# Mixture of experts on a Mamba/attention block: dense experts against tokens sorted into blocks of 128

## The chip, the core and the metric

The program runs on one NeuronCore of a Trainium2 chip. The core has five engines with their own instruction queues: TensorE (PE, matrix products, with its weight loads shown apart as PEld), VectorE (DVE), ScalarE (ACT), GpSimd (POOL) and SyncE (SP, which here only issues DMAs). The metric is the device time of one execution in microseconds (us), where less is better.

## The reference

The whole model is a state-space layer with a cross input, a quantised feed-forward layer, an attention layer and, last, a mixture of experts. Only the last layer is touched. x holds 4 batches of 512 tokens of 512 features, so 2048 tokens.

```python
scores = sigmoid(xt @ gate.T)                       # 2048 x 8
_, sel = top_k(scores + expert_bias, 2)             # two experts a token
top_scores = take_along_axis(scores, sel, axis=1)
order = argsort(sel.reshape(-1)); token_idx = order // 2; expert_ids = sel.reshape(-1)[order]
xb = (xt[token_idx] * top_scores[order]).astype(bfloat16)
for e in range(8):                                  # hidden size 256
    h = silu(xb @ w1[e].T) * (xb @ w3[e].T)
    oe = h @ w2[e].T
    out_r += where(expert_ids == e, oe, 0)
out = (silu(xt @ shared_w1.T) * (xt @ shared_w3.T)) @ shared_w2.T     # shared expert, f32
out = out.at[token_idx].add(out_r)
```

Here xt is the layer-normalised x, and the result is added to x. Each token is scaled by its score before it enters its two experts, so 4096 rows of work exist in all, out of the 16384 that eight experts on every token make.

## The kernel before

Everything ahead of the mixture of experts is one long schedule over the 4 batches. It ends with a last turn of attention, in which SP and POOL already load what the last layer needs: all expert weights in bf16 into `arena` (m_w1, m_w3, m_w2; POOL, L703), the shared expert's weights in f32 (into arena, wq and wo) and the first batch's x back from DRAM (`x3_load`, L544). The last SP load, s_w2 into wo, is issued after the last store of x.

The mixture of experts is then done batch by batch, 512 tokens at a time (`for_pairs`, L418, a loop over pairs of batches with the last pair written out). For a batch PE turns the normalised tokens into feature-major form (`xt_turned`, L1987: 4 groups of 4 transposes through PSUM tile pd, each drained by ACT at L1108), makes the 8 gate logits (32 records of 128x8, pd<-gateT,w2t), and ACT takes their sigmoid. DVE ranks the 8 biased scores of every token against each other (L1488 to L1505), and keeps a score where the rank is below 2 and zero elsewhere. So an expert that a token hasn't chosen sees that token as a zero row, and contributes zero.

For each expert e, DVE copies its gate column (`gcol`, L1508), PE spreads it over the partitions (`gates`, L2003, pd<-ident,gcol), DVE multiplies the whole batch by it into bf16 (`scaled_input`, L1512, 128x2048), PE computes the two up projections (`up`: 16 matmuls of 128x512), ACT applies Silu (L1120), DVE multiplies (L1518), and PE adds the down projection (`down`: 8 matmuls of 128x512) on top of what the shared expert and the experts before have left in the four PSUM banks `acc`. All matmuls go through the helper `mm`, L1548. The middle six experts stand in a hardware loop, where the weight address comes from a register. After the last expert DVE adds acc to x (L1541) and SP stores each quarter (L623). The next batch's layer norm (`moe_norm`) and transposes are woven into the last experts.

The order on each engine is the order in which the code of that engine's block is written. Nothing moves instructions between engines or reorders them; the engines meet at semaphores.

Of the kernel before, what the change touches and what calls it, by code (L numbers as in the profile page):

```python
# [13 lines left out]
BF16 = mybir.dt.bfloat16  # L14
ALU = mybir.AluOpType
# [4 lines left out]
P = 128  # L20
# [10 lines left out]
GH = 2  # L31
# [8 lines left out]
SAFE = 80.0  # L40

# [43 lines left out]
def program(nc, t):  # L85
    ctx = ExitStack()
    with ctx:
# [8 lines left out]
        x3_dram = nc.dram_tensor("x3_dram", (B, L, DM), F32).ap()  # L96
        kt_dram = nc.dram_tensor("kt_dram", (U_ALL, P, GH, L), F32).ap()
# [6 lines left out]
        tri = sb("tri", [P, E_, E_])  # L104
        minus_half = sb("minus_half", [P, 8])
# [108 lines left out]
        xbT = [qk_flat[:, i * NC * L:(i + 1) * NC * L].rearrange("p (c q) -> p c q", c=NC) for i in range(2)]  # L214

        x3 = [xs, xc]
        xn_moe = [w1t[:].rearrange("p c h -> p (c h)").bitcast(F32)[:, i * HID:(i + 1) * HID].rearrange("p (t d) -> p t d", t=NT) for i in range(2)]
        xnT_moe = [w2t[:].rearrange("p k d -> p (k d)").bitcast(F32)[:, i * HID:(i + 1) * HID].rearrange("p (c q) -> p c q", c=NC) for i in range(2)]
        gl = sb("gl", [P, 4, NT, E_])
        gcol = sb("gcol", [P, 2, NT])  # L220
        rk = sb("rk", [P, 2, E_, E_])
        hid_s = v_sb[:].rearrange("p t w -> p (t w)").rearrange("p (m q) -> p m q", m=MM)
        hid = [qkT_bf[:, i * HID:i * HID + MM * L].rearrange("p (m q) -> p m q", m=MM) for i in range(2)]
        sil = oT
        xo = hbuf[:, 1, 0:2 * DM].rearrange("p (s d) -> p s d", s=2)
# [9 lines left out]
        y_first = [ps[0], ps[1], po, pd]  # L235

# [65 lines left out]
        x3_in = [sem("x3_in0"), sem("x3_in1")]  # L302
# [7 lines left out]
        gb_full = sem("gb_full")  # L310
        gcol_done = sem("gcol_done")
        xb_done = sem("xb_done")
# [4 lines left out]
        xo_done = sem("xo_done")  # L317
        out_stored = [sem("out_stored0"), sem("out_stored1")]
# [99 lines left out]
        def for_pairs(eng, batch):  # L418


            with eng.Fori(0, B // 2 - 1) as j:
                for par in range(2):
                    batch(j * 2 + par, j, par, True)
            for par in range(2):
                batch(B - 2 + par, B // 2 - 1, par, par == 0)
# [10 lines left out]
        def _(sp):  # L436
# [4 lines left out]
                     (dtT, dram["dtT"]),  # L441
# [102 lines left out]
            def x3_load(b, par):  # L544
                sp.dma_start(x3[par][:], x3_dram[b].rearrange("(t p) d -> p t d", p=P)).then_inc(x3_in[par], 16)

            def turn(b, off, scan):
# [63 lines left out]
                sp.dma_start(x3_dram[b].rearrange("(t p) d -> p t d", p=P), xc[:]).then_inc(x3_stored, 16)  # L611
# [3 lines left out]
            sp.wait_ge(x3_stored, 16 * B + 16)  # L615

            def batch(b, j, par, follows):
                if follows:
                    sp.wait_ge(xo_done, NT * b + 1)
                    x3_load(b + 1, 1 - par)  # L620
                for k in range(NT):
                    sp.wait_ge(xo_done, NT * b + k + 2)
                    sp.dma_start(dram["out"][b].rearrange("(t p) d -> p t d", p=P)[:, k, :], xo[:, k % 2]).then_inc(out_stored[k % 2], 16)  # L623
            for_pairs(sp, batch)
            for i in range(2):
                sp.wait_ge(out_stored[i], 16 * B * NT // 2 + 16)
# [3 lines left out]
        def _(pool):  # L630
# [5 lines left out]
            def diagonals(s):  # L636

                if s == 0:
                    pool.wait_ge(const_in, 16 * 15)
# [44 lines left out]
            def turn(b, off, scan):  # L684
# [20 lines left out]
                def group(g):  # L705
                    G = b * NG + g
                    row_rms(G)
                    if is_first(g):
                        rstd(0 if scan else 3, 3 * b + 3)
                    if not scan:  # L710
                        expert_load(g)
# [3 lines left out]
            def batch(b, j, par, follows):  # L715
                if follows:
                    rstd(3, b + (3 * B + 1))
            for_pairs(pool, batch)


        @block.scalar
        def _(act):
# [139 lines left out]
            act.wait_ge(const_in, 16 * 15)  # L862
# [242 lines left out]
            def xt_out(b, par, k):  # L1105

                act.wait_ge(xt_full, b * NT + k + 1)
                nc.scalar.activation(xnT_moe[par][:, :, k * P:(k + 1) * P], pd[:].rearrange("p (c q) -> p c q", c=NC),  # L1108
                                     ACT.Copy).then_inc(xt_drained, 1)

            def batch(b, j, par, follows):
                X0 = b * (E_ + 1)
                act.wait_ge(logits_full, b + 1)
                nc.scalar.activation(gl[:, 0].rearrange("p t e -> p (t e)"), pd[:, 0:NT * E_], ACT.Sigmoid).then_inc(scored, 1)

                def silu(X):
                    for m in range(MM):
                        act.wait_ge(h1_full, 2 * X + m + 1)
                        act.wait_ge(hid_done, 2 * X + m + 1)
                        nc.scalar.activation(sil[:, m], px[0][:], ACT.Silu).then_inc(silu_done, 1)  # L1120
                silu(X0)
                with act.Fori(0, E_ - 1) as e:
                    silu(X0 + e + 1)
                if follows:
                    xt_out(b + 1, 1 - par, 0)
                silu(X0 + E_)
                if follows:
                    for k in range(1, NT):
                        xt_out(b + 1, 1 - par, k)
            for k in range(NT):  # L1130
                xt_out(0, 0, k)
            for_pairs(act, batch)
# [970 lines left out]
```

## Time and profile before

| | us |
|---|---|
| median of 3 runs | 2113.51 (2104.38 to 2113.51) |
| the profiled execution | 2109.74 |
| its span | 2108.1 |
| last layer in it, from the first transpose for it (1794.46) to the end | 313.6 |
| PE busy in the span | 1986.6 (94%) |
| mean granted TensorE clock | 0.963 of full |

The profile is of one execution, and its span is 1.6 us shorter than that execution's time. A busy PE includes the pipelined tail of a matmul, so two matmuls of 379 ns that start 0.215 us apart cost 0.215 us each. A granted clock of 1.00 is 2.4 GHz, one of 0.50 is 1.2 GHz. SPq stands for SP issuing a DMA; landing is when its semaphore has its last increment.

### The profile page before, as it was taken

Reading aid. Unit: us, or ns where it says so; the run is one execution under the profiler, and the core shown is the slowest. Engines: PE = TensorE matmul, PEld = TensorE weight load, DVE = VectorE, ACT = ScalarE, POOL = GpSimd, SP = SyncE. Lnnn points to the kernel's source line nnn. Section 1 sums busy time; section 2 is a strip of 40 time slices with the busy share of each in tenths; the row PEclk is TensorE's granted clock in tenths of the full one; section 3 lists DMA queues with packets and bytes.
Section 4 is the critical chain, followed back from the end, with each engine's and each line's share of the span. In section 5 each row is a group of like instructions: output and inputs, shape, how many; then the busy total and the mean of one; then the engine's idle time right before and its main releaser. Section 6 shows DMA issues by size and latency. Waiting matters only on the chain.

```text
span 2108.1 us, 24462 instructions
## 1 busy us (share of the span) xinstructions
PE 1986.6 (94%) x7508; PEld 1135.4 (54%) x7548; DVE 1462.6 (69%) x1762; ACT 1032.5 (49%) x2208; POOL 246.8 (12%) x124
## 2 busy tenths in 40 slices
PE   6899899999999989999998999988899999899998
PEld 2455445565654455656445665644556565454554
DVE  3799537999996699999758999993532333456554
ACT  4676435655653665656357655534444444121121
POOL 1002010111110021212001212100211010000000
PEclk8899899999999999999999999998999999999999
DMA  5264211222221122322202222222143332110100
GB/s 164 73 207 147 88 69 52 70 82 83 90 85 71 31 79 76 90 78 87 90 22 66 90 76 88 85 80 75 63 93 72 77 82 52 51 40 0 40 20 20
DMA packets 100788, 158.29 MB, mean 75 GB/s; under 512 B 9952, under 2 KB 53600, under 8 KB 100208
## 3 DMA queue, kind: packets, MB, share of 16 engines
q1 hardware_dynamic: 89136, 149.02, 22.0%
q0 software_dynamic: 10768, 6.82, 2.3%
q10 hardware_dynamic: 816, 1.57, 0.2%
q8 instruction: 40, 0.66, 0.1%
q14 instruction: 28, 0.23, 0.0%
HBM read 138.25 MB, written 25.43 MB: 78 GB/s over the span
## 4 chain that ended last, share of the span: by engine, by line
PE 60%; issue 25%; DVE 8%; ACT 3%; POOL 2%; DMA 1%; POOLq 0%; SPq 0%; ACTq 0%; DVEq 0%
PE ps L1548 21%; PE px L1548 13%; PE pp L1548 12%; PE po L1548 6%; PE pd L1548 6%; DVE arena L1212 2%; PE pp L1893 2%; DVE arena L1204 1%; ACT hbuf L1047 1%; ACT arena L783 1%; POOL rms_k L669 1%; DVE arena L1223 1%; POOL rms L660 0%; DVE xc L1404 0%; DVE arena L1230 0%
## 5 line engine op out<-in xcount | busy, mean ns | idle before, releaser
L1212 DVE TENSOR_TENSOR_SCAN arena<-arena 128x512 f32<-128x512 f32 x256 | 294.2, 1204 | 0.6
L1548 PE MATMUL ps<-qkT 128*128 128x512 f32 x512 | 256.4, 613 | 5.7 <-ACT hbuf L1047 3.0
L1047 ACT ACTIVATE hbuf<-ps,shift,rms_k 128x512 f32<-128x512 f32 x256 | 198.7, 778 | 123.8 <-PE ps L1548 116.2
L660 POOL TENSOR_TENSOR rms<-ssv,minus_half 128x4 f32<-128x4 f32 x64 | 154.0, 2407 | 808.5 <-ACT ssv L1023 808.5
L1548 PE MATMUL pp<-wq,xnT 128*128 128x256 f32 x1024 | 233.4, 382 | 2.9 <-issue 2.2
L1548 PEld LDWEIGHTS pp<-wq,xnT 128*128 128x128 f32 x1024 | 192.1, 190 | 41.0 <-issue 13.4
L1404 DVE SCALAR_TENSOR_TENSOR xc<-px,rden,xc 128x512 f32<-128x512 f32 x192 | 136.0, 738 | 85.0 <-PE px L1548 83.4
L1548 PE MATMUL px<-wo,oT 128*128 128x512 f32 x384 | 183.2, 599 | 0.7 <-DVE xc L1404 0.3
L783 ACT ACTIVATE arena<-arena,a_neg 128x512 f32<-128x512 f32 x256 | 163.3, 710 | 13.3 <-DVE arena L1190 7.3
L1548 PEld LDWEIGHTS ps<-qkT 128*128 128x128 f32 x512 | 91.7, 194 | 132.5 <-ACT hbuf L1047 70.6
L1548 PE MATMUL pp<-ctx_att,wk 128*128 128x512 f32 x256 | 134.3, 668 | 22.0 <-ACT ssv_k L845 6.4
L1120 ACT ACTIVATE oT<-px 128x512 f32<-128x512 f32 x72 | 43.0, 597 | 200.8 <-PE px L1548 200.8
L1548 PE MATMUL po<-hbuf,v_sb 128*128 128x512 f32 x256 | 130.7, 592 | 0.0
L1204 DVE TENSOR_TENSOR arena<-arena,bc 128x2048 f32<-128x2048 f32 x56 | 127.8, 2282 | 0.9 <-DVE v_sb L1172 0.6
L1548 PE MATMUL pd<-hbuf,v_sb 128*128 128x512 f32 x256 | 123.0, 603 | 0.0
L1223 DVE TENSOR_TENSOR arena<-arena,bc 128x2048 f32<-128x2048 f32 x52 | 118.8, 2284 | 0.0
L1336 DVE SCALAR_TENSOR_TENSOR hbuf<-px,fsc,ws 128x512 f32<-128x512 f32 x64 | 47.9, 750 | 98.4 <-PE px L1548 95.4
L1548 PE MATMUL ps<-wv,ctx_att 128*128 128x256 f32 x512 | 115.8, 379 | 0.0
L1230 DVE TENSOR_TENSOR arena<-arena 128x2048 f32<-128x2048 f32 x48 | 112.1, 2335 | 2.6 <-issue 0.3
L1418 DVE TENSOR_TENSOR dsum<-dsum,hbuf 128x512 f32<-128x512 f32 x128 | 88.6, 692 | 31.6 <-ACT hbuf L1047 25.6
L1548 PEld LDWEIGHTS ps<-wv,ctx_att 128*128 128x128 f32 x512 | 97.2, 190 | 13.4
L1548 PEld LDWEIGHTS px<-wo,oT 128*128 128x128 f32 x384 | 69.9, 189 | 58.9 <-issue 40.2
(211 smaller groups left out, 3087.0 us busy)
## 6 DMA issues: line engine op xcount, KB each, us to landing
bc<-bc_dram SPq DMA_DIRECT2D x56, 512.0 KB, 4.8
wo<-in_Wo SPq DMA_DIRECT2D x32, 512.0 KB, 3.6
wq<-in_Wq SPq DMA_DIRECT2D x32, 512.0 KB, 3.3
qkT<-kt_dram SPq DMA_DIRECT2D x32, 512.0 KB, 3.4
hbuf<-in_w SPq DMA_DIRECT2D x8, 1024.0 KB, 9.9
wk<-in_Wk SPq DMA_DIRECT2D x32, 256.0 KB, 2.8
wv<-in_Wv SPq DMA_DIRECT2D x32, 256.0 KB, 2.8
kt_dram<-xnT SPq DMA_DIRECT2D x14, 512.0 KB, 3.0
```

The lines of the kernel that those rows point to most:

```text
L660: nc.gpsimd.tensor_tensor(rms[:, j], ssv[:, j], half, ALU.pow).then_inc(rms_done, 1)
L783: nc.scalar.activation(dA[i][:, e], delta[:, e], ACT.Exp, scale=a_neg[:, e, bass.ds(g * GH + i, 1)]).then_inc(exp_done[i], 1)
L1047: nc.scalar.activation(pT[:, h, k], ps[s_use % 2][:], ACT.Exp, bias=shift[:, 0:1], scale=rms_k[:, bass.ds(G * (GH * NT) + (h * NT + k), 1) ...
L1120: nc.scalar.activation(sil[:, m], px[0][:], ACT.Silu).then_inc(silu_done, 1)
L1204: V.tensor_tensor(hb[i], du, bc_i[:, 0:1, :].broadcast_to((P, EC, L)), ALU.mult).then_inc(dbu_done[i], 1)
L1212: V.tensor_tensor_scan(hb[i][:, e], dA[i][:, e], hb[i][:, e], 0.0, ALU.mult, ALU.add).then_inc(scan_done[i], 1)
L1223: V.tensor_tensor(dst, hb[i], bc_i[:, 1:2, :].broadcast_to((P, EC, L)), ALU.mult).then_inc(hc_done[i], 1)
L1230: V.tensor_tensor(u, u, hb[i], ALU.add).then_inc(y_added, 1)
L1336: V.scalar_tensor_tensor(hbuf[:, k % 2, j * 512:(j + 1) * 512], bank, fsc[:, 0, 4, k:k + 1], ws1[:, j * 512:(j + 1) * 512], ALU.mult, ALU. ...
L1404: V.scalar_tensor_tensor(xc[:, k], px[bank][:], rden[:, h, k:k + 1], xc[:, k], ALU.mult, ALU.add).then_inc(px_drained[bank], 1)
L1418: V.tensor_tensor(dsum[:, h], dsum[:, h], pT[:, h, k], ALU.add).then_inc(ds_step[h], 1)
L1548: return nc.tensor.matmul(out, lhsT, rhs, start=first, stop=last, **kw)
```

## The change

The experts no longer see every token. Each token's two chosen experts are found as before, and then:

- `route_ranks` and `route_places` (DVE, with two small matmuls on PE, `places`) work out for each token its place among its expert's tokens. Each expert has its own region of 2048 + 128 rows in a DRAM tensor `xg_dram`.
- ACT scales the token-major rows by their score into bf16 (`routed_out`, 8 activations a batch), and POOL writes them to their places by indirect DMAs of 128 rows of 1 KB (`scatter`, 8 a batch, 32 in all). SP fills 128 rows behind each expert's last token with zeros.
- `block_tables` (DVE) turns the counts into a table: for each of 40 blocks of 128 rows, the expert's index (read into PE registers, six values for four blocks) and the first row (read into SP registers, four values for four blocks). 40 is the most that 4096 rows can need; unused blocks work on row 0 with expert 0.
- The 40 blocks run through a loop of ten turns with four blocks each. SP loads a block of 128x512 bf16 from xg_dram into one of four buffers, PE transposes it (`block_turned`), DVE copies it to SBUF (`block_x`), PE does the up projections (`block_up`: 16 matmuls of 128x128), ACT and DVE make the hidden values, PE does the down projection (`block_down`: 2 matmuls of 128x512), ACT copies it out as bf16 (`block_out`), SP stores it to `og_dram`.
- When all 40 blocks are stored, POOL gathers each token's two result rows (`gather`, 32 indirect DMAs), and DVE adds both to x (`final`).
- The shared expert is computed for batches 0 and 1 ahead of the blocks and for 2 and 3 behind them. All four batches of x are kept in SBUF. Layer norm of batch 1 moves into the last turn of attention, and two more constants are loaded at the start.

The core of the diff:

```diff
+NB = 40
+REGION = B * L + P
-                    x3_load(0, 0)
+                    for i in range(B - 1):
+                        sp.dma_start(x3[i], x3_dram[i].rearrange("(t p) d -> p t d", p=P)).then_inc(x3_in[i], 16)
...
+            def block_load(q, row):
+                sp.dma_start(xblk[q], xg_dram[bass.ds(row, P), :]).then_inc(xblk_in[q], 16)
+            def block_store(q, row):
+                sp.dma_start(og_dram[bass.ds(row, P), :], oblk[q]).then_inc(oblk_stored[q], 16)
+            rows = row_values(sp_tbl[0:1, 0, :])
+            for q in range(4):
+                block_load(q, rows[q])
+            def blocks(i, first, last):
+                if not last:
+                    rows = row_values(sp_tbl[0:1, bass.ds(i + 1, 1), :].rearrange("p o n -> p (o n)"))
+                for q in range(4):
+                    sp.wait_ge(bo_out, i * 4 + q + 1)
+                    block_store(q, i * (4 * P) + q * P)
+                    if not last:
+                        sp.wait_ge(bt_full, i * 4 + q + 1)
+                        block_load(q, rows[q])
...
+            def scatter(b):
+                for s in range(2):
+                    for k in range(NT):
+                        pool.wait_ge(routed_done, 2 * NT * b + s * NT + k + 1)
+                        nc.gpsimd.indirect_dma_start(
+                            out=xg_dram[:, :], out_offset=bass.IndirectOffsetOnAxis(ap=idx[:, b, s, k:k + 1], axis=0),
+                            in_=routed[b % 2][:, s, k], in_offset=None).then_inc(scattered[b % 2], 16)
...
+            for q in range(4):
+                pool.wait_ge(oblk_stored[q], 16 * NB4)
+            pool.wait_ge(table_step, TS + 4)
+            for b in range(B):
+                gather(b)
...
+            def block_out(j, slot, q, turns, head):
+                act.wait_ge(bo_full, j + 1)
+                if not head:
+                    act.wait_ge(oblk_stored[q], 16 * turns)
+                nc.scalar.activation(oblk[q], pp[slot][:], ACT.Copy).then_inc(bo_out, 1)
...
+            def final(b):
+                dve.wait_ge(g_in[b], 16 * 2 * NT)
+                dve.wait_ge(y_done, NT * b + NT)
+                for s_ in range(2):
+                    for k in range(NT):
+                        if s_:
+                            dve.wait_ge(fin_step, 2 * NT * b + k + 1)
+                        V.tensor_tensor(x3[b][:, k], x3[b][:, k], g_of[b][:, s_, k], ALU.add).then_inc(fin_step, 1)
...
+            hidden(2)
+            shared_out(2)
+            final(0)
+            hidden(3)
+            final(1)
+            shared_out(3)
+            final(2)
+            final(3)
...
+            def block_turned(j, slot, q, turns, head):
+                pe.wait_ge(xblk_in[q], turns)
+                for c in range(NC):
+                    m = nc.tensor.transpose(xT_ps[slot][:, c * P:(c + 1) * P], xblk[q][:, c * P:(c + 1) * P], ident_bf[:])
+                m.then_inc(bt_full, 1)
+            def block_up(j, slot, e, head):
+                pe.wait_ge(bt_out, j + 1)
...
+                for i, w in enumerate((m_w1, m_w3)):
+                    for m_ in range(MM):
+                        at_ = (i * MM + m_) * P
+                        for c in range(NC):
+                            m = mm(px[slot][:, at_:at_ + P], w[:, e, c, m_ * P:(m_ + 1) * P], xTs[slot][:, c * P:(c + 1) * P], c == 0, c == NC - 1,
+                                   skip_group_check=True)
+                m.then_inc(bh_full, 1)
+            def block_down(j, slot, e, head):
+                pe.wait_ge(bhid_done, j + 1)
...
+                for m_ in range(MM):
+                    m = mm(pp[slot][:], hT[slot][:, m_ * P:(m_ + 1) * P], m_w2[:, e, m_], m_ == 0, m_ == MM - 1)
+                m.then_inc(bo_full, 1)
+            def blocks(i, first, last):
+                e = expert_values(pe_tbl[0:1, bass.ds(i, 1), :].rearrange("p o n -> p (o n)"))
+                for q in range(4):
+                    if not (last and q == 3):
+                        block_turned(i * 4 + (q + 1), (q + 1) % 2, (q + 1) % 4, (i + (q + 1) // 4) * 16 + 16, first and q == 0)
+                    if not (first and q < 2):
+                        block_down(i * 4 + (q - 2), q % 2, e[q], first)
+                    block_up(i * 4 + q, q % 2, e[2 + q], first and q < 2)
```

On PE, in the loop over experts before, one expert begins like this. ISA is a register instruction that sets the weight address; qk_raw is the scaled input, arena the expert's weights.

```order
L2008 ISA [waits xb_done]
L1548 ISA [waits silu_done]
L1548 MATMUL px<-qk_raw,arena 128x512
L1548 ISA
L1548 MATMUL px<-qk_raw,arena 128x512
```

On PE in the loop over blocks now, one block's turn begins like this. hbuf is the loaded block in the transposes (po<-ident_bf,hbuf) and its transposed copy in the up projection (px<-hbuf,arena); dsum is the hidden value of an older block.

```order
L2363 MATMUL po<-ident_bf,hbuf 128x128 [waits bt_out,xblk_in2]
L2363 MATMUL po<-ident_bf,hbuf 128x128 x3
L1837 ISA [waits bo_out,bhid_done]
L1837 MATMUL pp<-arena,dsum 128x512
L1837 ISA
L1837 MATMUL pp<-arena,dsum 128x512
L1837 ISA [waits bhid_done,bt_out]
L1837 MATMUL px<-hbuf,arena 128x128
```

In the turn of block s, PE transposes block s+1, does the down projection of block s-2 and then the up projection of block s. The transposes wait for a load (xblk_in), and the down projection stands behind them in the queue.

On SP before, the loop over batches loads one batch of x and stores four quarters of another (xo_done is DVE's last addition).

```order
L614 DMA wo<-in_s_w2T 128x2x512
L421 UNCONDITIONAL_BRANCH [waits x3_stored]
L545 DMA xc<-x_dram 128x4x512 [waits xo_done]
L623 DMA out<-hbuf 128x512 [waits xo_done] x4
L545 DMA xs<-x_dram 128x4x512 [waits xo_done]
```

On SP now, one turn of the block loop begins like this; og_dram<-hbuf is a block's store, hbuf<-xg_dram the load of the block four further on.

```order
L674 TENSOR_LOAD wk
L702 ISA
L692 ISA [waits bo_out]
L692 DMA og_dram<-hbuf 128x512
L689 ISA [waits bt_full]
L689 DMA hbuf<-xg_dram 128x512
L702 REGISTER_ALU
```

A load is issued behind the store of the block four before it, and that store waits for the block's down projection to be copied out (bo_out).

## Rows read from the trace of the kernel before

**Rows 1.** page, part 1: busy us, share of the span, instructions
```profile
PE 1986.6 (94%) x7508; PEld 1135.4 (54%) x7548; DVE 1462.6 (69%) x1762; ACT 1032.5 (49%) x2208; POOL 246.8 (12%) x124
```

**Rows 2.** busy us of each engine by stretch; PEclk is the granted clock
```profile
core 0: us, PE busy (x) PEld busy (x) DVE busy (x) ACT busy (x) POOL busy (x), PEclk, DMA share, GB/s
1850.00:1900.00 50.00, 49.16 (x218) 25.86 (x220) 24.70 (x48) 11.73 (x19) 0.00 (x0) 0.97 0.12 42
1900.00:1950.00 50.00, 49.51 (x226) 24.18 (x230) 32.54 (x45) 10.48 (x18) 1.01 (x1) 1.00 0.00 0
```

**Rows 3.** timeline of one expert: start us, us, engine, line, operation, count
```profile
2067.14 2.84 PE L1548 MATMUL px<-qk_raw,arena 128*128 128x512 bf16 x12
2067.34 2.29 DVE L1512 TENSOR_TENSOR qk_raw<-w2t,pd 128x2048 bf16<-128x2048 f32 x1 [1.31 <-PE pd L2003]
...
2072.84 0.38 PE L1548 MATMUL px<-qk_raw,arena 128*128 128x512 bf16 x1
```

**Rows 4.** timeline: turning tokens, logits, shared up and down
```profile
1794.46 0.60 PE L1987 MATMUL pd<-ident,w1t 128*128 128x128 f32 x4
...
1795.84 0.63 PE L1987 MATMUL pd<-ident,w1t 128*128 128x128 f32 x4 [0.78 <-ACT w2t L1108]
...
1802.52 6.91 PE L1548 MATMUL pd<-gateT,w2t 128*128 128x8 f32 x32 [3.24 <-DMA wo<-in_s_w2T]
...
2030.70 3.74 PE L1548 MATMUL pd<-gateT,w2t 128*128 128x8 f32 x32 [0.69 <-ACT w2t L1108]
...
2039.50 1.88 PE L1548 MATMUL px<-w2t,wq 128*128 128x512 f32 x4
...
2057.57 2.74 PE L1548 MATMUL ps<-wo,v_sb 128*128 128x512 f32 x6
```

**Rows 5.** groups of instructions, 1815 to 2108: busy us, mean ns, idle before
```profile
L1120 ACT ACTIVATE oT<-px 128x512 f32<-128x512 f32 x72 | 43.0, 597 | 200.8 <-PE px L1548 200.8
...
L1518 DVE TENSOR_TENSOR qkT<-oT,po 128x512 bf16<-128x512 f32 x32 | 22.0, 687 | 23.5 <-PE po L1548 23.5
```

**Rows 6.** timeline of weight loads: fixed addresses, then addresses from a register
```profile
186.63 0.10 PEld L1548 LDWEIGHTS px<-ident_bf,qkT 128*128 128x128 bf16 x1
186.69 0.10 PEld L1548 LDWEIGHTS px<-minus_bf,qkT 128*128 128x128 bf16 x1
...
1838.75 0.10 PEld L1548 LDWEIGHTS px<-qk_raw,arena 128*128 x1 [0.40 <-issue]
1838.87 0.10 PEld L1548 LDWEIGHTS px<-qk_raw,arena 128*128 x1
1839.00 0.10 PEld L1548 LDWEIGHTS px<-qk_raw,arena 128*128 x1
```

**Rows 7.** DMA issues: engine, count, KB each, median us from issue to landing
```profile
wq<-in_Wq SPq DMA_DIRECT2D x32, 512.0 KB, 3.3
...
wk<-in_Wk SPq DMA_DIRECT2D x32, 256.0 KB, 2.8
...
out<-hbuf SPq DMA_DIRECT2D x16, 256.0 KB, 2.2
...
arena<-in_m_w3T POOLq DMA_DIRECT2D x8, 256.0 KB, 5.7
...
bc_dram<-arena SPq DMA_DIRECT2D x4, 64.0 KB, 1.6
...
gateT<-in_gateT SPq DMA_DIRECT2D x1, 16.0 KB, 2.0
```

**Rows 8.** timeline: SP's issue of a load that had waited for PE
```profile
1727.49 0.59 PE L1548 MATMUL pp<-wq,xnT 128*128 128x256 f32 x2
...
1728.28 0.37 SPq L470 DMA_DIRECT2D wq<-in_Wq  x1
```

**Rows 9.** busy us by stretch, where PE waits often
```profile
50.00:60.00 10.00, 4.55 (x36) 3.88 (x36) 9.79 (x7) 7.82 (x10) 0.00 (x0) 0.58 0.57 174
260.00:270.00 10.00, 6.45 (x17) 3.77 (x16) 0.00 (x0) 1.44 (x3) 0.00 (x0) 0.50 0.58 180
```

**Rows 10.** timeline: POOL's issues of direct loads
```profile
1730.64 0.79 POOL L703 DMA_DIRECT2D arena<-in_m_w1T  x1
1731.42 0.76 POOL L703 DMA_DIRECT2D arena<-in_m_w3T  x1
```

More of the change, by code:

```diff
@@ L14 @@
 BF16 = mybir.dt.bfloat16
+I32 = mybir.dt.int32
 ALU = mybir.AluOpType
@@ L416, in is_last, with for_blocks @@
             return isinstance(g, int) and g == NG - 1
[L418 to L425, printed above, removed]
+        def for_blocks(eng, blocks):
+            blocks(0, True, False)
+            with eng.Fori(1, NB4 - 1) as i:
+                blocks(i, False, False)
+            blocks(NB4 - 1, False, True)
         def for_groups(eng, group):
@@ L624, in _, with row_values @@
-            for_pairs(sp, batch)
-            for i in range(2):
-                sp.wait_ge(out_stored[i], 16 * B * NT // 2 + 16)
+            def row_values(ap):
+                _, values = nc.values_load_multi_w_load_instructions(
+                    ap, engines=[mybir.EngineType.SP], min_val=0, max_val=E_ * REGION - P,
+                    skip_runtime_bounds_check_because="rows are worked out from counts of at most B * L tokens an expert")
+                return values
+            sp.wait_ge(zero_set, 1)
@@ L1113, in batch @@
                 act.wait_ge(logits_full, b + 1)
[L1114 to L1123, printed above, removed]
@@ L2062, in _ @@
+            for b in range(2):
+                xt_turned(b)
+                logits(b)
+            places(0)
             pe.wait_ge(mw_in, 16 * (3 * E_ + 1))
-            pe.wait_ge(sw_in, 32)
             for i in range(2):
@@ L2067, in _ @@
                 pe.wait_ge(px_drained[i], turn_of(B - 1, OFF_LAST)[0]["px"] + HALF_LAST["px"])
-            for_pairs(pe, batch)
+            up(0, 0)
+            up(0, 1)
+            places(1)
+            down(0)
+            for b in range(2, B):
+                xt_turned(b)
+                logits(b)
+            places(2)
+            up(1, 0)
+            places(3)
+            pe.wait_ge(gate_step, GS * 3 + 13)
+            pe.wait_ge(y_done, NT)
+            mm(acc[3][:, 0:E_], ones[:], before[:, B * NT], True, True).then_inc(count_full, 1)
@@ new lines, in _, with expert_values @@
+            up(1, 1)
+            down(1)
+            def expert_values(ap):
+                _, values = nc.values_load_multi_w_load_instructions(
+                    ap, engines=[mybir.EngineType.PE], min_val=0, max_val=E_ - 1,
+                    skip_runtime_bounds_check_because="the count of experts that end by a block, times whether the block is one of theirs")
+                return values
+            def block_turned(j, slot, q, turns, head):
+                pe.wait_ge(xblk_in[q], turns)
+                if not head:
+                    pe.wait_ge(bt_out, j - 1)
+                for c in range(NC):
+                    m = nc.tensor.transpose(xT_ps[slot][:, c * P:(c + 1) * P], xblk[q][:, c * P:(c + 1) * P], ident_bf[:])
+                m.then_inc(bt_full, 1)
```

562 lines of the change are left out of this document (390 added, 172 removed).

## The prediction, made before the changed kernel ran

> **What bounds the kernel now.** I read the page's part 1 first: PE is busy for 94% of the span [rows 1]. By stretches the last layer is no different: PE 49.2 and 49.5 us of 50 at a clock of 0.97 and 1.00, DVE 25 to 33, ACT 11 [rows 2]. So in this layer every microsecond taken off PE counts, if nothing takes its place. The timeline then gives the price of its parts. One expert on one batch: its twelve first matmuls start at 2067.14, those of the next expert at 2072.84, so 5.70 us [rows 3], and DVE's 2.29 us scaling lies beside them. 8 experts x 4 batches x 5.70 = 182 us of the 313.6 us from 1794.46 to the end. The other 131 us are turning tokens, logits, the shared expert and the end.
>
> **What goes.** All 182 us, gate spreading and scaling included. Before, the first logits also waited 3.24 us for s_w2, in the row of 1802.52 [rows 4]; now only `down` waits for it.
>
> **The blocks: what one costs PE.** With a fixed weight address a load and a matmul of 128 columns start 0.06 us after the pair before; with an address from a register the weight loads start 0.12 and 0.13 us apart [rows 6]. In the old loop 0.12 was hidden, because a matmul of 512 columns lasts 0.215 us. Now it isn't: 16 x 0.125 = 2.0 us for the up projections. The transposes (fixed) take 4 x 0.06 = 0.25, the down projection 2 x 0.215 + 0.1 = 0.5, waits and registers 0.2: 3.0 us a block. For 40 blocks that is 120 us against 182. ACT needs 0.60 for copying 512 columns out [rows 5] and about 0.4 for Silu on 256; DVE about 0.65 and 0.45. Neither decides.
>
> **The blocks: what one costs in latency.** The load of block j+4 is issued only after the store of block j, which waits until block j's down projection is copied out. PE does that down projection in the turn of block j+2 and wants block j+4 at the start of the next turn; the down projection of block j+1 stands behind those transposes. So from one down projection to the next there is a closed circle:
> - transposes 0.25, down 0.5, the array's tail 0.2 (a matmul of 215 ns is shown as 379), a wake-up 0.1: 1.05 us at full clock;
> - ACT's copy 0.60 [rows 5];
> - SP awake 0.2 us after the last releaser (PE ended at 1728.08, the issue began at 1728.28), the store's issue 0.37 [rows 8], the second wait and register 0.1: 0.7;
> - the load, from issue to landing. 512 KB take 3.3, 256 KB 2.8, 16 KB 2.0 [rows 7]. 128 KB on that line are 2.3 to 2.4; with a store of 128 KB just ahead of it in the same queue I take 2.5.
>
> Sum 4.85 us. The up projections (2.0 us) lie inside the load's time. The clock raises it: in stretches where PE is busy for 4.6 or 6.5 us of 10, the granted clock was 0.58 and 0.50, which is the 1.2 GHz level for most or all of it [rows 9]. Here PE would be busy for 3.0 of 4.9 us. At half clock transposes and down take 0.7 us more; with a part of that I take P = 5.0 us a block. Bounds: 2.0 for the load and full clock, 4.2; 2.9 for the load and half clock all the way, 5.9. PE reads six register values from SBUF every four blocks, and SP four. No row shows such a read; between nothing and the smallest load that a row has (2.0 us), it fits into PE's 2.0 us of waiting a block, so I take 0 and keep 0 to 0.5 us a block.
>
> The Trainium skill ("TensorE: Matmul & The Clock Gate", HAM oscillation) says that a matmul loop which waits for a DMA in every turn keeps falling back to 1.2 GHz. Rows 9 agree that the clock falls where PE waits. Followed fully it would make P 5.5 us and the time 2175. The same notes ("DMA: Bandwidth & Descriptors", Latency and other measured facts) give a register load from memory a floor of about 600 ns, and "Runtime: NRT & Kernel Launch" about 200 ns a register; by that estimate PE's six are 1.2 us, hidden at P = 5.0 and showing only if PE bounds.
>
> From the first block's transposes to the end of the last down projection: 5 us to the first down, 36 P = 180 (the last four blocks need no further load), 5.5 for the last turns. 190 us, against 182 before. The 62 us that PE is spared turn into waiting.
>
> **Ahead of the blocks.** Everything from 1794.46 is now serial on PE: 4 batches turned at 4 x 1.40 us = 22 (1794.46 to 1795.84 is one [rows 4]); logits 3.7 to 6.9 us each [rows 4], 4 x 6 = 24, the clock being low behind them; shared expert of batches 0 and 1, up 32 records and down 16, eight records in 3.4 us [rows 4], 20.6 a batch = 41. Added waits: down(0) behind DVE's `route_places`(1) and `hidden`, 3.5; places and counts, handing pd back, 4; down(1) behind DVE's table (20 small operations of some 0.25 us), 3. Half clock on part of this, 7. Sum 105, so PE could begin the blocks at 1899. Queued behind these waits are only the blocks. The old kernel wove turning and ranking into its experts, where it cost little. Layer norm of batch 1 in the last turn of attention is hidden by DVE's idle half; the other cover, three loads of 1 MB in place of one, lies ahead of loads that are due 20 us later. Two more constants at the start: two issues, +1.
>
> POOL's indirect DMAs appear in no row. A direct one costs POOL 0.79 us to issue [rows 10] and lands after 5.7 when three are queued [rows 7]; I take 1.2 us each, nearer to the direct one, bounds 0.8 and 2.5. Then the 8 of a batch are 10 us. By the same sum the places of batch 3 are known at 1887; POOL is at batch 2 until 1889, ends batch 3 at 1899, which lands 2.5 later, and reading rows and loading the first block take 4 more: 1905. So the scatter sets the start, 111 us after 1794.5, bounds 95 to 125.
>
> **Behind the blocks.** PE computes the shared expert for batches 2 and 3: 2 x 20.6 + 2 x 0.9 of waiting for `hidden` = 43. POOL begins to gather when the last store has landed, 0.65 + 0.2 + 1.8 = 2.7 us after the last down projection (64 KB stored in 1.6, 256 KB in 2.2 [rows 7]); 32 x 1.2 = 38, landed at 43.5. DVE adds in its written order: final(1), 8 x 0.69 = 5.5 [rows 5], stands ahead of shared_out(3), which ends at 45.5; final(2) and final(3) 5.5 each, 56.5; the last store 2.2 [rows 7]: 58.7.
>
> **Sum.** 1794.5 + 111 + 190 + 58.7 + 1 = 2155 of span, against 2108. With 1.6 outside it, 2157; the runs shown lie from 5 under to 4 over the profiled execution, so 2157 stands as the forecast: 47 us or 2.2% slower. The change would pay only with P below 3.7 us.
>
> **Rivals.**
> - *PE bounds the blocks, faster.* The load lands before PE wants it, so P is PE's own 3.0 to 3.3 us. For it: 3.0 us of PE work a block is well counted, and DMA queues are nearly empty here (DMA share 0.12 and below [rows 2]). Against: the circle above needs the load to land in 0.7 us, and no load in rows 7 is below 2.0. It decides wherever the circle is below 3.7. Time: 36 x (5.0 - 3.0) = 72 less, 2085. Chance 0.14; with partial forms, 0.18.
> - *GpSimd bounds the ends, slower still.* An indirect DMA costs 2.5 us. The scatter of the last batch ends 18 us later, the gather takes 80 us instead of 38, so the last addition ends at 93 instead of 58.7: 2157 + 52 = 2209. For it: 128 separate rows each, made by an engine that needs 0.79 us even for a plain load. Against: nothing measured. Chance 0.13.
> - *Even.* P of 3.6 to 3.9 with the rest as summed: 2106 to 2118. Chance 0.06.
>
> My forecast has 0.63. Its own range is 2125 to 2195 (36 x 0.9 us on the block price, 15 on the front, combined). The range given, 2095 to 2210, adds the nearer part of both rivals. Slower by over 0.5% (about the smallest change a measurement of this kernel tells) 0.76, within 0.06, faster 0.18.
>
> **What would show it.** In the block stage the transposes (po and pd from ident_bf) idle on the DMA hbuf<-xg_dram, 4.2 to 5.9 us apart, PE busy for 60% and a clock well below 1. Wrong if they are about 3 us apart with no wait for a DMA: then the load's path was too dear. The chain at the end should be DVE additions behind the gather; if POOL issues are above 1.55 us each, they set the end. The front should last 95 to 125 us from the first transposes for this layer to the first block. The forecast is wrong as a whole if the span from the first block to the last down projection is below 145 us.

## The result, and the profile after

The changed kernel takes 2143.49 us (median of 4, 2141.89 to 2147.66) against 2112.14 for the kernel before beside it: a ratio of 1.0159, 95% interval 1.013 to 1.0189. It is slower, by 1.6% where 2.2% was forecast. The profiled spans are 2142.3 and 2108.1 us. PE is busy for less time and waits more:

```profile
PE 1940.1 (91%) x7519; PEld 1144.1 (53%) x7551; DVE 1399.0 (65%) x1759; ACT 1047.2 (49%) x2252; POOL 309.6 (14%) x189
```

That is 46 us less of busy PE than in [rows 1], and 34 us more of span. By stretches, the block stage:

```profile
core 0: us, PE busy (x) PEld busy (x) DVE busy (x) ACT busy (x) POOL busy (x), PEclk, DMA share, GB/s
1900.00:1950.00 50.00, 33.45 (x244) 24.23 (x245) 10.85 (x28) 9.23 (x20) 0.00 (x0) 0.69 0.18 56
1950.00:2000.00 50.00, 30.96 (x227) 22.55 (x230) 8.13 (x22) 10.43 (x22) 0.00 (x0) 0.69 0.19 58
2000.00:2050.00 50.00, 31.91 (x232) 23.27 (x232) 7.65 (x21) 10.51 (x22) 0.00 (x0) 0.66 0.19 58
```

Where [rows 2] had PE at 49 us of 50 and a clock of 0.97 and 1.00, it now has 31 to 33 at 0.66 to 0.69. What it waits for is in the answer for the transposes of the blocks:

```profile
its engine sat idle before it (us, times) until:
  DMA hbuf<-xg_dram: 114.5, 66
  issue: 15.1, 8
  DVE wv L1761: 4.9, 2
```

The 114.5 us are of two rows that wait side by side, the matmuls and their weight loads. The view of the loads (`xg_dram`) tells them apart:

```profile
  PE pd L2363: 30.4, 19
  PE po L2363: 30.4, 18
```

So PE itself waited 60.8 us for loads, in 37 waits. One turn of the circle follows, with the lines of weight loads and of VectorE left out:

```profile
1993.77 0.60 PE L2363 MATMUL pd<-ident_bf,hbuf 128*128 128x128 bf16 x4 [1.50 <-DMA hbuf<-xg_dram]
1994.17 1.06 PE L1837 MATMUL pp<-arena,dsum 128*128 x2
1995.02 1.91 PE L1837 MATMUL px<-hbuf,arena 128*128 128x128 bf16 x16
1995.35 0.60 ACT L1271 ACTIVATE hbuf<-pp 128x512 bf16<-128x512 f32 x1 [2.66 <-PE pp L1837]
1996.12 0.36 SPq L692 DMA_DIRECT2D og_dram<-hbuf  x1
1996.66 0.33 SPq L689 DMA_DIRECT2D hbuf<-xg_dram  x1
...
1998.86 0.40 PE L2363 MATMUL po<-ident_bf,hbuf 128*128 128x128 bf16 x4 [1.93 <-DMA hbuf<-xg_dram]
1999.31 0.38 PE L1837 MATMUL pp<-arena,dsum 128*128 x1
1999.73 0.60 ACT L1271 ACTIVATE hbuf<-pp 128x512 bf16<-128x512 f32 x1 [2.38 <-PE pp L1837]
2000.50 0.35 SPq L692 DMA_DIRECT2D og_dram<-hbuf  x1
```

Read it as a chain: transposes at 1993.77, ACT's copy 1.58 later, store 0.77 later, load 0.54 later, the next transposes 2.20 later, 5.09 us in all, with down at half clock (1.06 for two matmuls). The next turn has them at full clock (one of the two records is missing), and ACT's copy follows after 0.87 instead of 1.58: a turn that is 0.71 shorter, 4.4 us. The up projections (1.91) end long before the load has landed. The first row below gives the starts of the first and the last of the 40 stores, the others the DMAs' times from issue to landing (the last number):

```profile
L692 SPq DMA_DIRECT2D og_dram<-hbuf x40: 332/355/361, 1910.9 to 2086.4; - x40
```

```profile
hbuf<-xg_dram SPq DMA_DIRECT2D x40, 128.0 KB, 2.1
og_dram<-hbuf SPq DMA_DIRECT2D x40, 128.0 KB, 1.7
```

The last three intervals need no load and are 5.8 us together; the 36 before are 169.8 us, 4.72 each. The two ends of the last layer follow: GpSimd's last eight scatters (the second number is the median in ns), then from the timeline the start of the blocks and the end.

```profile
L807 POOL DMA_INDIRECT xg_dram<-qkT,wv x8: 956/956/978, 1890.0 to 1898.8; - x8
```

```profile
1901.86 1.94 SPq L689 DMA_DIRECT2D hbuf<-xg_dram  x4
...
1903.78 0.19 DVE L1761 TENSOR_TENSOR wv<-wk,wv 128x32 int32<-128x32 f32 x1
1904.05 0.38 PE L2363 MATMUL po<-ident_bf,hbuf 128*128 128x128 bf16 x4 [2.03 <-DVE wv L1761]
...
2089.09 0.99 POOL L814 DMA_INDIRECT w1t<-og_dram,wv  x1 [189.29 <-DMA og_dram<-hbuf]
2090.39 0.96 POOL L814 DMA_INDIRECT w1t<-og_dram,wv  x1 [0.30 <-issue]
...
2121.32 0.69 DVE L1769 TENSOR_TENSOR v_sb<-oT,po 128x512 f32<-128x512 f32 x1 [6.12 <-PE po L1837]
...
2121.93 4.99 DVE L1783 TENSOR_TENSOR ws<-ws,w1t 128x512 f32<-128x512 f32 x8
...
2128.08 0.94 POOL L814 DMA_INDIRECT qk_raw<-og_dram,wv  x1 [0.30 <-issue]
...
2129.86 4.90 DVE L1783 TENSOR_TENSOR bc<-bc,w2t 128x512 f32<-128x512 f32 x8
2134.67 4.90 DVE L1783 TENSOR_TENSOR xc<-xc,qk_raw 128x512 f32<-128x512 f32 x8
```

An indirect DMA takes POOL 0.95 us and the next starts 0.30 later: 1.25 to 1.27 from one to the next. The last addition ends 11.5 us after the last gather is issued. The row of 1904.05 names VectorE's L1761 as what PE waited for, but in the kernel PE waits there for the first load and for the table of blocks. The table was done at 1892.31 (L1749) and the load landed at 1903.92, so it was the load.

### The profile page after: what moved, and what is told of

It reads as the page before. It is cut to its first block, busy times and chain, and to the rows that moved or that the text cites. A ratio compares the mean times of both kernels' runs of the same rounds, so it can differ in the third digit from the quotient of the medians.

```text
span 2142.3 us, 25171 instructions
## 1 busy us (share of the span) xinstructions
PE 1940.1 (91%) x7519; PEld 1144.1 (53%) x7551; DVE 1399.0 (65%) x1759; ACT 1047.2 (49%) x2252; POOL 309.6 (14%) x189
## 4 chain that ended last, share of the span: by engine, by line
PE 62%; issue 16%; DVE 10%; ACT 5%; DMA 4%; POOL 1%; SPq 1%; ACTq 0%; DVEq 0%; POOLq 0%
PE ps L1837 20%; PE pp L1837 14%; PE px L1837 13%; PE pd L1837 7%; PE po L1837 5%; DMA hbuf<-xg_dram 4%; DVE arena L1368 2%; PE pp L2182 2%; DVE arena L1360 1%; ACT hbuf L1271 1%; ACT hbuf L1160 1%; ACT arena L896 1%; DVE arena L1379 1%; SPq L692 1%; PE pd L2281 1%
## 5 line engine op out<-in xcount | busy, mean ns | idle before, releaser
L1144 ACT ACTIVATE qk_raw<-pp,rms 128x128 f32<-128x128 f32 x256 | 72.9, 368 | 48.8 <-POOL rms L746 48.5
```

What stands on the lines that cost most here:

```text
L1144: m = nc.scalar.activation(qraw[:, k, h * D:(h + 1) * D], pp[bank][:, i * GW + h * D:i * GW + (h + 1) * D], ACT.Copy, scale=rms[:, j, h, i ...
```

## The experiments

My theory was the circle: block j+4's load stands behind block j's store in SP's order. Its rivals were a slow DMA path whoever asks for it, PE's work or its clock, and GpSimd at the two ends. The kernel before ran beside each group of kernels. It took 2107.2 us beside the first four kernels, and 2107.5 to 2109.3 beside the others. The first four ran on one chip (A), the next seven on another (B), the last on a third (C); which one had the changed kernel's own run isn't known. That matters below.

**Loads ahead of stores.**

```
 for q in range(4):
-    sp.wait_ge(bo_out, i * 4 + q + 1)
-    block_store(q, i * (4 * P) + q * P)
     if not last:
         sp.wait_ge(bt_full, i * 4 + q + 1)
         block_load(q, rows[q])
+    if not (first and q < 2):
+        sp.wait_ge(bo_out, i * 4 + q - 1)
+        block_store((q + 2) % 4, i * (4 * P) + (q - 2) * P)
...
```

(Behind the loop, the last two blocks are stored.)

> SyncE's loop is turned round: it loads block j+4 as soon as block j is turned, and stores block j-2 behind it, so that no load waits for a store of its own or a later block. Circle theory (the block period of 4.7 us is down, ACT's drain, SP's store and load issues and the load's 2.1 us landing, one behind the other): the circle opens, the waits of the block transposes on the loads vanish, and the period falls to TensorE's own work, 0.25 to 0.5 for turning, 0.5 for down, 2.0 for up and 0.15 to 0.2 for its share of the register load that is now bare: 3.0 to 3.3 us. 36 periods x 1.5 us = 50 to 60 us less than the changed kernel: about 2085 to 2095 us, below the kernel before. Rival 1 (the loads are late because the DMA queue or the memory is slow, whoever asks): the period stays above 4.3 us and the time above 2128. Rival 2 (TensorE's half clock in this stage sets the period): the clock stays at 0.65 to 0.70 and the period at or above 4.3 us.

Measured: 2083.94 us, 0.9895 of before (0.9873 to 0.9916). The stores, the transposes' waits, and the engines by stretch:

```profile
L692 SPq DMA_DIRECT2D og_dram<-hbuf x40: 332/355/362, 1911.0 to 2027.9; - x40
```

```profile
  issue: 20.7, 18
  DMA hbuf<-xg_dram: 3.2, 3
```

```profile
1950.00:2000.00 50.00, 44.82 (x354) 32.62 (x357) 12.32 (x33) 16.18 (x33) 0.00 (x0) 0.90 0.27 85
```

That is 1 us below the band I gave. The stores are 39 intervals of 3.00 us instead of 4.50 (here and below all 39 are counted alike). The row for the DMA fell from 114.5 to 3.2 us, and PE's own part of it from 60.8 to 2.6, though a load still takes 2.0 to land and 85 GB/s are moved instead of 58. So the DMA path was not slow, it was asked late. The clock rose from 0.69 to 0.90 once PE had work, with nothing changed but SP's order. Both rivals fall.

**The load ahead of the store, with the same waits.**

```
 sp.wait_ge(bo_out, i * 4 + q + 1)
-block_store(q, i * (4 * P) + q * P)
 if not last:
     sp.wait_ge(bt_full, i * 4 + q + 1)
     block_load(q, rows[q])
+block_store(q, i * (4 * P) + q * P)
```

> The waits of SyncE's loop stay as they are; only the issue of the load of block j+4 stands ahead of the store of block j. Circle theory: the store's issue and the step behind it (0.35 + 0.2 us) leave the circle, so the period falls by 0.5 us (4.7 to 4.2) and the time by 36 x 0.5 = 18 us, to about 2125 us. Rival (TensorE's work or its clock sets the period): nothing changes, 2143 +- 4 us.

Measured: 2126.58 us, 1.0087 of before (1.007 to 1.0104), 16.9 less than the changed kernel.

```profile
L692 SPq DMA_DIRECT2D og_dram<-hbuf x40: 333/356/1362, 1915.0 to 2070.2; - x40
```

The 39 intervals take 155.2 us, 3.98 each against 4.50: one issue out of the circle is worth 0.52 us a block, as in the chain above (store to load, 0.54). Nothing else was changed, so the circle is closed through SP's order, and taking out a part shortens it by that part. The block stage is 20.3 us shorter and the whole only 16.9, because in the profiled execution the blocks began 3.6 us later (1907.64 for 1904.05). That was late already in the work ahead of them: ACT's wait of 5.8 us for the logits ended at 1865.19 instead of 1861.61.

**Gate and up weights at a fixed address, alone and with the loads ahead.**

```
-m = mm(px[slot][:, at_:at_ + P], w[:, e, c, m_ * P:(m_ + 1) * P], ...
+m = mm(px[slot][:, at_:at_ + P], w[:, 0, c, m_ * P:(m_ + 1) * P], ...
```

All blocks then go up through expert 0, whatever their own expert is.

> The gate and up weights of every block are read at expert 0's fixed address instead of at the register's (so all blocks go up through expert 0; down keeps its register). TensorE's 16 matmuls of a block take about 0.9 to 1.1 us instead of 2.0. Circle theory: the up step lies beside the load's landing, so the period stays within 0.2 us of 4.7 and the time within 8 us of 2143 (2135 to 2147). Rival (TensorE's work sets the period): the period falls by 0.9 us to 3.8, the time by 33 us to 2110.

> Both at once: loads ahead of stores, and gate and up weights at expert 0's fixed address. Circle theory: with the circle open TensorE's work counts, so the fixed address now gives what it gave nothing for alone: 0.7 to 1.0 us a block below the loads-ahead kernel, a period of 2.0 to 2.4 us, a time of about 2050 to 2065 us. Rival (something beside TensorE, as the chain turn, copy, up, silu, multiply, down, sets the period at 3 us or more once the loads are in time): the same time as loads ahead alone.

Measured: 2133.90 us alone (1.0123, 1.0106 to 1.014), 2028.28 us with the loads ahead (0.9629, 0.9604 to 0.9653). The stores, alone and then together:

```profile
L692 SPq DMA_DIRECT2D og_dram<-hbuf x40: 332/355/362, 1909.3 to 2081.5; - x40
```

```profile
L692 SPq DMA_DIRECT2D og_dram<-hbuf x40: 332/355/412, 1910.3 to 1972.4; - x40
```

Alone the interval goes from 4.50 to 4.42; with the loads ahead from 3.00 to 1.59. The same edit is worth 0.08 us a block inside the circle and 1.41 outside it. That is the plainest proof of what bounds which kernel. Two sizes missed. Alone the median fell 9.6 us, 1.6 beyond my band. In the profiled executions the block stage gave 3.4 of it and the work ahead 1.6; the rest isn't in that execution, which took 2139.38. Together I expected 2050 to 2065, having priced the address at 0.9 us a block.

The 1.41 us are not all the address. With the loads ahead, three transposes of four start 2.6 to 3.0 us apart and the fourth about 3.99, because PE's queue stands still for 1.35 us at the turn of the loop (its branch, the load of six registers of 0.59, some register steps). With the fixed address too, the intervals are 1.55 to 1.70 and the fourth 1.73: the same turn, with a register load of 0.75, lies beside matmuls that are already queued. So about 1.2 us of the 1.41 are the weights' addresses, and the other 0.2 to 0.3 is the turn of the loop, now hidden.

**Half the gathers.** GpSimd fetches only the rows of the first choice, and the additions use them twice:

```
-for s in range(2):
+for s in range(1):
     for k in range(NT):
         nc.gpsimd.indirect_dma_start(out=g_of[b][:, s, k], ...
```

> The changed kernel with 16 indirect gathers instead of 32: the rows of the second choice are not fetched, and the final additions take the first choice's rows twice. GpSimd is done 20 us earlier. Theory (the end is set by the shared expert's chain of batches 2 and 3 on TensorE and by VectorE's order behind it; the last gather lands only just in time at 2130 us): final(2) still starts 44.4 us after the last block, so the time moves by 0 to 1.5 us, 2142 to 2144. Rival (GpSimd's gathers set the end, as the case of slow indirect DMAs in the prediction had it): the time falls by 5 to 20 us. A little in between would say that the landing of batch 3's rows is what final(3) waits for.

Measured: 2152.85 us (1.0225, 1.0201 to 1.0249): above the changed kernel, which neither theory nor rival had. From the last store's issue to the end it is 55.9 us (2090.4 to 2146.3) with 16 gathers, as with 32 (2086.4 to 2142.3). So GpSimd doesn't set the end, which was the question. The extra time was at another place, below.

**Eight blocks' experts in one register load** (on top of loads ahead; PE's loop over 8 blocks, its table of 10 values a row).

```
-for q in range(4):
+for q in range(8):
     ...
-        block_down(i * 4 + (q - 2), q % 2, e[q], first)
-    block_up(i * 4 + q, q % 2, e[2 + q], first and q < 2)
+        block_down(i * 8 + (q - 2), q % 2, e[q], first and q < 4)
+    block_up(i * 8 + q, q % 2, e[2 + q], first and q < 2)
```

> The loads-ahead kernel with TensorE's table of experts read for eight blocks at a time (10 registers a load, 5 loads in the loop) instead of for four (6 registers, 10 loads). In the loads-ahead trace TensorE stands still for 1.25 us at each load, where a block's turning starts 4.0 us after the one before instead of 2.75. If the price is that of a load: 5 x 1.25 = 6 us less, 2078 us. If it is that of a register (60 before, 50 now): 1.25 / 6 x 10 = 2 us less, 2082 us. If the stall has nothing to do with the load (a jump of the loop, say) it also halves with the count of turns of the loop, as in the first case, which this run can't tell apart.

Measured: 2116.98 us (1.0045, 1.0028 to 1.0062). PE's register loads, first in the loads-ahead kernel, then in this one, and its stores:

```profile
L2357 PEldq TENSOR_LOAD <-wk x9: 588/592/612, 1914.8 to 2013.9; - x9
```

```profile
L2357 PEldq TENSOR_LOAD <-wk x5: 1081/2412/2427, 1940.6 to 2037.9; - x5
```

```profile
L692 SPq DMA_DIRECT2D og_dram<-hbuf x40: 332/356/362, 1925.9 to 2043.1; - x40
```

The 39 intervals take 117.2 us against 116.9: no gain where I expected 2 to 6 us. There are half as many loads, of 10 values each. They alternate: three of the five take 2.4 us and the two between them 1.08, instead of 0.59. Rows of the table now start 40 bytes apart and not 32; whether that makes every second load long wasn't tested.

**Another order of additions at the end** (on top of loads ahead).

```
 final(0)
-hidden(3)
+hidden(3, (0,))
 final(1)
-shared_out(3)
+hidden(3, (1,))
 final(2)
+shared_out(3)
 final(3)
```

> The loads-ahead kernel with another order on VectorE at the end: final(1) goes between the two halves of hidden(3), and final(2) ahead of shared_out(3), both in gaps of 6 us in which VectorE stood still. The last batch's rows land 44.6 us after the last block and shared_out(3) is done by 44.3, so the last additions end at 49.5 and the store at 51.7 instead of 56.8: 5 us less, 2079 us. Rival (the gathers land later than I read them, or the order delays TensorE's chain by more than it gives): within 2 us of 2084.

> Loads ahead, eight blocks' experts a load, and the new order at the end, together; nothing is left out of the computation. The three act in different places (each block, each loop turn, the end) and should add up: 2084 - 6 - 5 = 2073 us, 1.6% below the kernel before. If one hides another (the register load was partly beside something else, or TensorE's chain at the end moves with the clock), 2076 to 2080.

Measured: 2112.82 us (1.0024, 1.0011 to 1.0036) and 2112.41 us (1.0022, 1.0006 to 1.0037), 34 and 39 us over expectation. The piece that the order touches did what it should: from the second product of hidden(3) to the end it is 21.0 us in the changed kernel (2121.32 to 2142.3) and 16.3 in both of these (2094.49 to 2110.8, 2091.67 to 2108.0), 4.7 less. No median shows that gain: on this chip the loads-ahead kernel without the new order took 2107.62 (below), and the one with it 2112.82.

**Weights moving, tokens loaded** (with the three edits above).

```
-for m_ in range(MM):
-    at_ = (i * MM + m_) * P
-    for c in range(NC):
-        m = mm(px[slot][:, at_:at_ + P], w[:, e, c, m_ * P:(m_ + 1) * P], xTs[slot][:, c * P:(c + 1) * P], ...
+for c in range(NC):
+    m = mm(px[slot][:, i * MM * P:(i + 1) * MM * P], xTs[slot][:, c * P:(c + 1) * P], w[:, e, c], ...
...
+for m_ in range(MM):
+    m = nc.tensor.transpose(hT_ps[slot][:, m_ * P:(m_ + 1) * P], hmid[slot][:, m_ * P:(m_ + 1) * P], ident_bf[:])
```

> As the three together, but gate and up are computed with the tokens' block as the loaded operand and the expert's weights as the moving one: 8 matmuls of 256 columns instead of 16 of 128 whose loaded operand stood at the register's address; the product then needs two more turnings of 128x128 and a copy of 128x256 on VectorE before down. Nothing is left out. If the cost of the register's address is that of each loaded weight tile (0.125 us apart instead of 0.056), a block loses 16 x 0.125 = 2.0 us and gets 8 x 0.11 + 0.2 = 1.1 us: 0.9 us less a block, 40 x 0.9 = 36 us less, about 2040 us, unless the longer way (turn, copy) leaves a wait of 0.2 to 0.4 us in each block (then 2048 to 2055). Rival (a register's address costs the same wherever it stands, for each column that it moves): no gain, 2073 us or more.

Measured: 2096.58 us (0.9937, 0.9919 to 0.9955). That is 15.8 under the three together beside it, where 36 less was expected, and far over the 2040 to 2055 expected of the time.

**What was late in the last five.** The traces of these five have a place at about 1898 us where VectorE starts 9 us after the matmul that it waits for should have ended, though PE's own records run on at their usual spacing. All but the half-gather kernel have a second place near the end, where ACT and VectorE wait for the shared expert's products: from the last block store to the end they take 18 to 24 us longer than the loads-ahead kernel's 55.9 (less the 4.7 where the order is new). To tell chip from program:

> The loads-ahead kernel once more, beside the next. The last five kernels were all 8 to 35 us over what was expected of them, and their traces show why only in part: TensorE's results come 9 us late at 1898 us (VectorE waits for the last gate and up product), and in four of the five 21 us late behind 2064 us, while the block stage between runs as expected. They ran on another chip than the first four. If the late results belong to that chip, this kernel has them wherever the next one has them, and takes about 2112 us there, or neither has them and it takes 2084 us again. If they belong to the changes of the last kernels (the order of the program, its length), this kernel takes 2084 us whether the next one is late or not.

> The kernel with the weights as the moving operand once more, on the same chip as the loads-ahead kernel. Chip theory: its stalls (9 us at 1898 us and about 20 us near the end) are there or away together with those of the loads-ahead kernel: about 2096 us with them, about 2066 to 2070 us without; the difference to the loads-ahead kernel is 15 to 18 us in both cases. Program theory: 2096 us, above the loads-ahead kernel's 2084.

> The changed kernel itself once more, to compare the kernels of the last three calls with. Chip theory: if it falls on the chip on which TensorE's results came late, it has the 9 us at 1898 us, as the kernel with half the gathers had there (2152.9), and up to 15 us more near the end, where the full 32 gathers run beside the shared expert: 2153 to 2168 us; on another chip it takes 2143 us as before. Rival (the half-gather kernel was slower for a reason of its own): 2143 us on any chip. The block period is 4.7 us in every case.

Measured: loads ahead on chip B 2107.62 us (1.0009, 0.9994 to 1.0024) where it had 2083.94 on A; weights moving 2086.83 (0.9916, 0.9888 to 0.9943), with both late places, where 2096 was expected with them and 2066 to 2070 without; the changed kernel, on C, 2148.08 (1.0186, 1.0166 to 1.0206), with none of the late places. The changed kernel with all its gathers was not run on B, and why the half-gather kernel has only the first place isn't explained. The loads-ahead kernel on A has no such wait; on B:

```profile
ACT oT L1246 <- remote: 36.8, 2, 29.6
DVE v_sb L1773 <- remote: 27.2, 2, 19.7
```

("remote" is a release that nothing in the trace explains.) SP is slow at the first place too, where it issues the eight stores of zeros; A, then B:

```profile
L682 SPq DMA_DIRECT2D xg_dram<-dsum x8: 332/337/529, 1889.6 to 1893.7; - x8
```

```profile
L682 SPq DMA_DIRECT2D xg_dram<-dsum x8: 3/356/695, 1885.9 to 1898.4; - x8
```

The block stage is the same on both: 116.9 us for 39 intervals. The kernel before shows none of it in its times on B. What the late places have in common isn't settled. The executions also reach the last layer at different times: ACT's wait for the logits ended at 1861.63 in the loads-ahead kernel on A and at 1857.69 on B. The first store on B is at 1915.1 for 1911.0, so the first place cost 8.1 us and not 4. Counted so, it cost 10.4 to 10.6 in the kernels with half the gathers, eight a load, new order and three together.

So the loads-ahead kernel's gain of 23 us over before is that of chip A, and it is nothing on B. On B the weights-moving kernel was 20.8 us below it. Of the 18.9 between the profiled executions, 16.5 are 39 intervals of 2.57 instead of 3.00 (stores from 1911.0 to 2011.4) and 4.1 lie ahead of the first store; from the last store to the end it took 1.7 longer (72.0 for 70.3), so the 4.7 of the new order is not to be seen there. It is the best version that leaves nothing out: 0.6% and 0.8% under the kernel before in its two measurements, both on the chip with the late places. The medians of these two are 9.8 us apart, and their profiled executions differ by 9.2 us ahead of the first store (1920.2 and 1911.0). So a difference of a few microseconds between separate measurements on this chip says little.

## Why the prediction was right, and where it was off

The prediction was right in direction and in mechanism. Its steps follow, each against the profiled execution. The total, 2155.2 of span, was 12.9 us too high: P accounts for 10, the front and the end for 1.7 and 1.9, the start of the layer for 0.7, and the first and last turns, longer than assumed, give 1.5 back.

- **The circle: right.** Its mechanism is shown by the first two experiments, and its rival (PE bounds the blocks) by the fixed address. The term was mis-sized: P is 4.72, not 5.0, and 36 x 0.28 = 10 us. The load was it: I took 2.5 between the 2.8 of 256 KB and the 2.0 of 16 KB [rows 7], with an addition for the store ahead of it; it lands in 2.1 whether a store is ahead or not. SP's 0.7 for two issues was 0.17 + 0.54, and ACT's 0.60 as in [rows 5]. The lower bound of 4.2 is mis-added: its own terms (1.05, 0.60, 0.7, 2.0) make 4.35. Nothing rests on it.
- **The clock: half right.** I took a part of half clock; the stage has 0.66 to 0.69, and single turns of 4.4 and 5.1 us side by side. The Trainium skill ("TensorE: Matmul & The Clock Gate", HAM oscillation) says that a loop waiting for a DMA in each turn falls back to 1.2 GHz again and again. The trace agrees that it falls, but not all the way: 5.5 us a block by that rule alone, 4.72 measured. With the wait gone the clock was 0.90.
- **PE's 3.0 us a block: right**, though hidden here. With the loads ahead a block takes 2.8 (from transposes to transposes in the timeline) and 3.00 with the loop's turns, for which the prediction had nothing.
- **Registers at nothing: right, and for the reason given.** They lay in the wait. When the wait goes they cost: each fourth interval of the transposes is 3.99 instead of 2.8. Of these 1.2 us, the load of six values is 0.59, the rest the loop's branch and register steps around it. The floor of 600 ns for a load in the Trainium skill ("DMA: Bandwidth & Descriptors", Latency and other measured facts) fits the 592 ns of the row. The about 200 ns a register of the Trainium skill ("Runtime: NRT & Kernel Launch", Instruction fetch mechanics) would make the load 1.2 us, twice what the trace has. That the whole stall is 1.2 us too proves nothing for it: beside busy matmuls the same load adds about 0.2.
- **The front: 111 forecast, 109.3 measured** (1794.75 to 1904.05). The scatter does set it: its last DMA is issued at 1898.84, the first load at 1901.86, and that lands at 1903.92. VectorE is in a dead heat with it: it ends the gathers' addresses (L1761), which stand ahead of its first block copy, at 1903.97. An indirect DMA was taken at 1.2 and is 1.26 (seven steps from 1890.0 to 1898.8).
- **The end: 58.7 forecast, 56.8 measured.** The gathers take 39.0 from the first issue to the last, not 38; the additions take 4.9 a batch, not 5.5: eight of 0.69 start 0.60 apart. The shared expert on PE and then VectorE's order set the end, as said: half the gathers changed nothing, and another order made that piece 4.7 us shorter. The sign that issues above 1.55 us would set the end is loose: by the forecast's own times (the last additions start at 51, a gather lands in 2.5) it is 1.43. At 1.25 there were 3 us to spare.
- **The rivals.** GpSimd at 2.5 us a DMA: refuted by the rows. PE as the bound: refuted here, and true of the kernel with the loads ahead. Its 2083.94 is within 1.1 us of the 2085 worked out for the rival, in part by luck: that sum had the ends 3.6 us too long, and on chip B the same kernel took 2107.62.

## What to carry to other kernels

When work is cut into small steps that are loaded and stored one by one, draw the circle from "buffer free" to "next load landed" and write every queue's program order into it: here the order of two lines in SP's loop cost 1.5 us a block, 60 us in all, while the kernel without it is only 23 us under the kernel before, and that on one chip. Buffers alone don't help (there were four) if the load stands in its queue behind a wait for something younger than what frees its buffer. And price an edit only after asking what bounds the stage: the same edit was worth 0.08 us a block before the circle was opened and 1.41 after. Last, run a kernel again before crediting a few microseconds to an edit: here the same kernel differed by 24 us between two chips and by 9.8 between two measurements on one.

## What the runs showed of the hardware

- An indirect DMA of 128 rows of 1 KB costs GpSimd 0.95 us and 0.30 to the next, scatter or gather. In the changed kernel scatters landed 2.4 to 2.6 us after their issue, most gathers after 2.6 to 2.8 and single ones after 4.4.
- An expert's address from a register costs about 1.2 us a block for 16 loaded tiles (0.125 us apart instead of 0.056), and another 0.2 to 0.3 because the loop's turn is then no longer hidden. With 8 matmuls of 256 moving columns, two more transposes and a copy, the block was 0.43 us shorter; not the 0.9 expected.
- A granted clock below 1 can be a consequence alone: it rose from 0.69 to 0.90 with no edit but the order of SP's waits and issues.
- Register loads on PE of 6 values took 0.59 us (0.75 beside busy matmuls); of 10 values, by turns 1.08 and 2.4.
- Chips differ by more than a tuning step. One of three held up results of PE at two places of this program: in the loads-ahead kernel's profiled executions 8.1 us ahead of the blocks, half of it masked by an earlier start of the layer, and 14.4 behind them (70.3 for 55.9), with 24 between the medians. The kernel before took 2107.2 to 2109.3 on all three. Both places have indirect DMAs on GpSimd beside float32 matmuls of the shared expert at full clock, but so has the same program on the other chips.
